# Two graph attention layers on one core: a second form of the second attention, powers for the norms' roots, loops of eight graphs

## What is computed

```python
def layer0(src, adj, ...):
    scores = einsum('bhid,bhjd->bhij', q, k) / sqrt(32)
    attn = softmax(scores, axis=-1)
    out = sum(einsum('bhij,bhjd->bhid', attn * (adj == r), v_r) for r in range(4))
    x = ln(src + out @ Wo + bo, g1, beta1)
    return ln(x + gelu(x @ W1 + b1) @ W2 + b2, g2, beta2)

def layer1(features, adj, Wq, Wk, Wv, Wffn, g1, b1, g2, b2):
    q, k, v = heads(features @ Wq), heads(features @ Wk), heads(features @ Wv)
    e = einsum('whqd,whkd->whqk', q, k)
    e = where(e >= 0, e, 0.2 * e)
    attn = softmax(where(adj[:, None] > 0, e, -9e15), axis=-1)
    h = einsum('whqk,whkd->whqd', attn, v)
    out = ln(h, g1, b1)
    out = ln(concatenate([out, features], axis=-1) @ Wffn.T, g2, b2)
    return out + features
```

## Time and profile before

| | us |
|---|---|
| runs | 3582.01, 3583.69 (median), 3592.45 |
| profiled execution | 3597.16 (its span 3594.9) |
| first attention, from the start to its barrier | 0 to 1250; first matmul 26.50, last output 1239.21 |
| feed-forward | 1250 to 1985 |
| second attention | 1985 to 3594.9, 1610; first matmul 2011.47 |

### The profile page before, as it was taken

One profiled execution on the slowest core, in us unless ns is written; L12 is line 12 of the kernel. 1 busy time (PEld: TensorE's weight loads), 2 busy tenths in 40 slices (PEclk: granted clock), 3 DMA queues, 4 the chain that ended last, 5 costly groups with the idle time before them and its releaser, 6 DMA issues. The chain is left out here.

```text
span 3594.9 us, 96982 instructions
## 1 busy us (share of the span) xinstructions
PE 3085.4 (86%) x31169; PEld 2287.0 (64%) x31169; DVE 2723.2 (76%) x7645; ACT 2427.9 (68%) x5646; POOL 1769.1 (49%) x3716
## 2 busy tenths in 40 slices
PE   5999999999999489999999488878888888788886
PEld 3666666666665256666666377767777777677775
DVE  4888888888888345655555388888888888888886
ACT  2566666666666255555555488888888888888886
POOL 0566666666666425545545034443444444344445
PEclk9999999999999789999999699998999999999998
DMA  3444444444444111111111344443443444344332
GB/s 117 131 133 132 132 132 132 132 132 132 132 132 124 42 47 48 54 52 47 47 47 38 94 113 115 118 114 102 114 119 103 112 115 115 100 113 119 106 109 60
DMA packets 296923, 364.46 MB, mean 101 GB/s; under 512 B 29536, under 2 KB 213728, under 8 KB 296544
## 3 DMA queue, kind: packets, MB, share of 16 engines
q1 hardware_dynamic: 295104, 358.20, 33.6%
q10 hardware_dynamic: 1440, 1.65, 0.1%
HBM read 241.77 MB, written 117.96 MB: 100 GB/s over the span
## 5 line engine op out<-in xcount | busy, mean ns | idle before, releaser
L433 ACT ACTIVATE l_prob<-l_neg_e,l_neg_max 128x256 f32<-128x256 f32 x1024 | 518.0, 522 | 18.0 <-DVE l_neg_max L726 10.2
L726 DVE CUSTOM_DVE_ANT_0 l_neg_e<-l_score,l_leaky 128x256 f32<-128x256 f32 x1024 | 391.7, 420 | 151.0 <-ACT l_prob L433 93.1
L896 PE MATMUL l_tprob<-l_ident,l_prob 128*128 128x128 f32 x2048 | 362.3, 304 | 157.8 <-ACT l_prob L433 146.8
L473 ACT ACTIVATE l_leaky<-l_score 128x512 f32<-128x512 f32 x512 | 307.6, 601 | 219.8 <-PE l_score L912 219.6
L1774 DVE TENSOR_TENSOR f_gl<-f_act,f_gh 128x512 f16<-128x512 f32 x256 | 244.9, 957 | 275.5 <-ACT f_act L1701 275.4
L909 PE MATMUL l_score<-l_stack 128*128 128x256 f16 x1024 | 283.3, 299 | 107.0 <-DMA l_stack<-qk_scratch 106.9
L1696 ACT ACTIVATE f_gh<-f_up,f_b 128x512 f16<-128x512 f32 x256 | 175.5, 685 | 279.1 <-PE f_up L1822 279.0
L1387 DVE TENSOR_TENSOR a_linked<-a_prob,a_mask 128x1024 f32<-128x1024 f32 x256 | 350.2, 1368 | 6.9 <-ACT a_prob L1211 6.9
L732 DVE TENSOR_TENSOR l_pt<-l_tprob,l_pt 128x512 f16<-128x512 f32 x512 | 351.1, 686 | 1.4 <-ACT l_pt L446 1.4
L896 PEld LDWEIGHTS l_tprob<-l_ident,l_prob 128*128 128x128 f32 x2048 | 235.9, 151 | 174.7 <-ACT l_prob L433 130.2
L543 POOL TENSOR_TENSOR l_hl<-l_zt,l_hh 128x512 f16<-128x512 f32 x64 | 74.0, 1156 | 507.6 <-ACT l_hh L493 507.6
(11 more groups left out here) (227 smaller groups left out, 10376.2 us busy)
## 6 DMA issues: line engine op xcount, KB each, us to landing
l_stack<-qk_scratch SPq DMA_DIRECT2D x512, 128.0 KB, 3.1
a_stack<-qk_scratch SPq DMA_DIRECT2D x384, 128.0 KB, 2.8
qk_scratch<-a_qk SPq DMA_DIRECT2D x64, 512.0 KB, 2.8
qk_scratch<-l_qk SPq DMA_DIRECT2D x64, 512.0 KB, 4.7
a_x_sb<-x_t SPq DMA_DIRECT2D x64, 256.0 KB, 2.7
a_adj_sb<-adj_t SPq DMA_DIRECT2D x64, 256.0 KB, 2.8
a_res<-x_nodes SPq DMA_DIRECT2D x64, 256.0 KB, 3.0
after_attention<-a_z_out SPq DMA_DIRECT2D x64, 256.0 KB, 2.1
```

The costliest lines, as they stand in the source:

```text
L433: last = nc.scalar.activation(prob[:, s, i], src[:, i], ACT.Exp, bias=neg_max[:, s, i:i + 1], scale=1.0 if first else -1.0, accum_out=rsum ...
L473: nc.scalar.activation(leaky4[:, s], score[s][:], ACT.Relu, scale=1.0 / ALPHA - 1.0).then_inc(relu_done, 1)
L726: last = nc.vector.tensor_tensor_reduce(neg_e[:, s, i], score[s][:, i], leaky4[:, s, i], -ALPHA, 3e38, ALU.add, ALU.min, neg_max[:, s, i:i ...
L896: last = nc.tensor.transpose(tprob[s][:, jt, it * P:(it + 1) * P], prob[:, s, it, jt * P:(jt + 1) * P], ident[:])
```

## The change

**The second attention** gets its own function `attention_second` (prefix `b_`), in the form of the first attention:

- the stack of 98 rows in a ring of four, with six loads for eight; x in four slots, and xh, xl kept for eight graphs;
- upright scores `score` without the mask; VectorE adds the mask (16-bit, from `adj`) and takes the maximum in one pass (`neg_max`, two instructions of 128x256 a head); no relu on this side;
- per graph `offset` (the maximum with the leaky factor, times 5), turned by TensorE (`turn_max`), split into two 16-bit rows (`max_rows`, times 1/4096), stored and loaded into rows 96 and 97 (`store_m`);
- turned scores `score_t` (`ST`), then a relu with factor 4 in place in PSUM on ScalarE (`relu`), then `add` on TensorE into the same bank: `far` times an identity with 5 * -9e15 (128x512, 16-bit), and the 98 rows again, scores and maximum; then one exponential of 128x512 with factor 0.2 into `prob`, float32;
- `values` and `sums_t` in column tiles, as in the first attention, four groups per graph; `turn_sum`, `rinv`, `turn_heads`, `hs`; 
- for rows without edges: `linked` (from `adj_t`, loaded in addition), `count` (two matmuls with ones), `any`, `far = any - linked` on GpSimd, and `zero_q` (q's halves times `any`, on VectorE, before the store);
- v is kept as float32 (one copy by ScalarE, no halves); `hl` moves from GpSimd to VectorE; the factor g1 is multiplied into `wo` at the start, its bias into a row that is added with `y`.

**The norms** of all three stages: one `ALU.pow` with exponent -0.5 on GpSimd and the product `shift`; VectorE has two small operations behind the statistics in place of five.

**The loop**: U is 8, so the body is eight graphs (eight pairs in the feed-forward) and `2 * U` = 16 are written out ahead of it. x has four slots and the stack a ring of 4 in `attention_first`, as many as before.

```diff
-U = 4
-RSQRT_MAGIC = float(0x5F3759DF)
-NEWTON = 3
+U = 8
...
                 def norm_root(b, k):
...
-                    for _ in range(NEWTON):
-                        for out, a, c in ((s["prod"], s["half"], s["root"]), (s["prod"], s["prod"], s["root"])):
-                            nc.gpsimd.tensor_tensor(out[:], a[:], c[:], ALU.mult).then_inc(root_chain[k], 1)
...
+                    nc.gpsimd.tensor_tensor(s["root"][:], s["var"][:], minus_halves[:], ALU.pow).then_inc(root_chain[k], 1)
+                    pool.wait_ge(root_chain[k], count(b, ROOTS, 1))
                     nc.gpsimd.tensor_tensor(shift[k][:], s["neg_mean"][:], s["root"][:], ALU.mult).then_inc(root_chain[k], 1)
...
-    RING = U
+    RING = 4
+    XS = 4
...
+def attention_second(nc, x_in, x_out, adj, adj_t, w, scr, scr_m, consts):
...
+    AT = {"load": 4, "load_adj": 4, "xT": 8, "xh": 9, "xl": 9, "q": 10, "q_hi": 11, "q_lo": 11, "linked": 8, "k": 12, "k_hi": 13, "k_lo": 13,
+          "count": 9, "any": 9, "v": 14, "v_out": 15, "zero_q": 12, "far": 10, "store_qk": 13, "mask": 16, "S": 17, "max": 17,
+          "offset": 24, "turn_max": 25, "max_rows": 26, "store_m": 26, "ST": 28, "relu": 28, "add": 29, "exp": 29, "values": 33, "res": 45,
+          "evac": 40, "turn_sum": 40, "rinv": 41, "turn_heads": 43, "hs": 43, "stats0": 44, "z1": 45, "turn_z": 46, "hh": 46, "hl": 47,
+          "out_x": 47, "out": 48, "y": 49, "stats1": 50, "z": 52, "affine": 53, "store": 55}
...
+                        sp.dma_start(scr[i].rearrange("k p n -> p k n"), qk[:, i]).then_inc(qk_stored[i], 16)
+                        sp.wait_ge(qk_stored[i], parts_stored)
+                        if stacks_read is not None:
+                            sp.wait_ge(added, stacks_read)
...
+                        nc.scalar.activation(prob[:, he], score_t[s][:].rearrange("p t n -> p (t n)"), ACT.Exp,
+                                             scale=ALPHA).then_inc(exp_done, 1)
...
+                        nc.scalar.activation(score_t[s][:], score_t[s][:], ACT.Relu, scale=SLOPE - 1.0).then_inc(relu_done, 1)
...
+                        for it in range(NT):
+                            col = column(hm, it)
+                            last = nc.vector.tensor_tensor_reduce(junk[:, s, it], score[s][:, it], mask[:, i, it], -1.0, 3e38,
+                                                                  ALU.add, ALU.min, neg_max[:, i, col:col + 1])
...
+                        nc.tensor.matmul(score_t[s][:].rearrange("p t n -> p (t n)"), far_ident[:], far[:, r4].rearrange("p t n -> p (t n)"),
+                                         start=False, stop=False, skip_group_check=True)
+                        for jt in range(NT):
+                            last = nc.tensor.matmul(score_t[s][:, jt], stack[0:KS, r4, 1, a, c * N + jt * P:c * N + (jt + 1) * P],
+                                                    stack[0:KS, r4, 0, a, c * N:(c + 1) * N], start=False, stop=True, skip_group_check=True)
+                        last.then_inc(added, 1)
...
+                        for term in range(2):
+                            for a in range(HQ):
+                                he = HQ * c + a
+                                part = slice(DH * a, DH * (a + 1))
+                                if term:
+                                    last = nc.tensor.matmul(sums_t[part, 0:N], pick[:, c], prob[:, he, cols], start=k == 0, stop=k == 3)
+                                else:
+                                    nc.tensor.matmul(heads_t[part, c], values[:, r4, jt, he * DH:(he + 1) * DH], prob[:, he, cols],
+                                                     start=jt == 0, stop=jt == 1)
...
-    attention_layer(nc, 1, mid2, out, adj, w1, scr1, consts)
+    attention_second(nc, mid2, out, adj, adj_t, w1, scr1, scr_m, consts)
```

728 lines of the change are left out of this document (654 added, 74 removed).

## The result

The changed kernel takes 3394.6 us (median of four runs, 3390.4 to 3399.7) against 3584.8 before (3582.0 to 3592.5): a ratio of 0.947, 95% interval 0.945 to 0.949. That is 190 us less; the prediction said 164 less, 3420 us.

The account below looks back on a forecast made before the run. TensorE bound the first attention and feed-forward; in the second attention no engine was full, TensorE waiting for exponentials and stack. Stages -163, -6 and +5 gave -164: 3433 against the profiled 3597.2, 3420 us as median; range 3340 to 3525.

Parts of the forecast that it names:

- TensorE's sum: Second attention: TensorE's operations, each priced from trace rows, add up to 20.2 us a graph at clock 1.00.
- Late stack: Second attention: TensorE waits 0 to 1.9 us a graph for the stack from scratch memory; 0.6 taken.
- late v: Second attention, step 6 of a graph's eight: v waits 0.4 us for k low.
- The stage's sum: Second attention: start, 64 graphs of 21.2 us, fill and drain, and five branches, together 1447 against 1610 us, -163.
- Start, fill and drain: Second attention: TensorE starts 20 us after the barrier, and filling and draining the pipeline take 45 us.
- -38 for the power: First attention: power in place of Newton's chain saves some 0.6 us a graph over 64 graphs, -38 us.
- xl is then bound by xh: First attention: without Newton's chain xl waits for xh, ending 0.7 us before the chain's end; 0.6 of 0.73 saved.
- +32 in the first attention: First attention, eight-graph body: five branches back of 4 us, +20, and a sometimes late stack, +12.
- +5: Feed-forward with a body of eight: one branch back and its start cost 5 us.
- The second: Rival, both attentions: no late stack, branches of 2 us, second attention's period 20.4 us; 3340 us, chance 0.14.
- The third: Rival: bodies beyond the buffer slow both attentions, +96 in the first, +147 in the second; 3660 us, chance 0.06.
- The fourth: Rival: power takes 3 us or more, so z1 is late in each graph, +1.5 x 64; 3515 us, chance 0.05.
- The first: Rival: the stack binds each graph of the second attention at 22.1 to 22.8 us; say 3500 us, chance 0.18.

Follow-up runs that it names:

- Newton's run: The changed kernel with Newton's chain and its seeds back in the second attention alone, the other stages keeping the power: 3609.5 us.
- the eight loads: The changed kernel with two more loads of the second attention's stack per graph, into rows nothing reads, so eight for six: 3485.8 us.
- the shorter body: The kernel before with two of three products left out of the second attention's values, loop of four, 1310 TensorE instructions for 1820: 3481.0 us.

## Why the prediction was right, step by step

**TensorE's sum** held. 20.2 us were forecast for a graph of the second attention; the window has 20.2 (957.8 over the 47.5 graphs of 21.0 us that 1000 us hold), and as much without a loop (991.5 over 49.2), where a graph takes 20.3 us. The clock of 1.00 came too. Relu in place costs 0.50 us start to start and the power 0.71, both near the value taken:

```profile
2635.59 0.71 POOL L1888 TENSOR_TENSOR b_nw_root<-b_nw_var,b_minus_halves 128x2 f32<-128x2 f32 x1 [13.25 <-DVE b_nw_neg_mean L1961]
...
2637.34 0.60 ACT L1821 ACTIVATE b_prob<-b_score_t 128x512 f32<-128x512 f32 x1 [0.82 <-PE b_score_t L2098]
2637.84 0.59 ACT L1827 ACTIVATE b_score_t<-b_score_t 128x512 f32<-128x512 f32 x1
2638.35 1.08 ACT L1873 ACTIVATE b_z<-b_y,b_shift,b_nw_root 128x256 f32<-128x256 f32 x2
```

**Late stack and late v.** 0.6 and 0.4 were forecast; the rows have 0.3 and nothing. The store was hardly ever late (4 of 48), since a fetch falls into its first 2 us in 2 of 48 graphs. That was luck: the prediction named the fetching at changing places but worked out nothing from it, and in the kernel before the same fetching hit every store.

**The stage's sum** was right by two errors that offset each other. 64 graphs and five branches were 1382 us by the prediction; 64 times the measured mean from y to y (20.60) is 1319, 63 less. In the loop a graph with its share of the branch is 21.0 where the prediction has 21.2 and 0.4: a branch back was priced at 5 us, and TensorE stands 2.3 to 2.7 at it. The rest of the 63 is that the first ten graphs take 20.3 us and the last four 14 to 19. Start, fill and drain were 65 and are 111 (some 5 more, counted from the barrier). The first y comes 121 us behind the stage's first load (105 before), the last 12 us ahead of its end (15 before): the longer pipeline was priced by its steps at full pace, and its start costs more.

**The first attention.** -38 for the power was 36 in the run with the power alone, by another way. The step that failed is "xl is then bound by xh, 0.7 us before the chain's end": one pair of rows was read, and in the graph ahead of it the two lie 0.16 apart. With the chain gone GpSimd waits for xh, and then the four operations ahead of `hl` are what TensorE waits for:

```profile
609.17 1.16 POOL L1285 TENSOR_TENSOR a_xl<-a_x_sb,a_xh 128x512 f16<-128x512 f32 x1 [3.21 <-ACT a_xh L1209]
610.29 1.27 POOL L1297 TENSOR_TENSOR a_resb<-a_res,a_vrow 128x512 f32<-128x512 f32 x1
611.51 2.26 POOL L1309 TENSOR_TENSOR a_z<-a_z,a_vrow 128x512 f32<-128x512 f32 x1
613.86 1.28 POOL L1313 TENSOR_TENSOR a_z_out<-a_z,a_vrow 128x512 f32<-128x512 f32 x1
615.09 2.14 POOL L1276 TENSOR_TENSOR a_hl<-a_heads_n,a_hh 128x512 f16<-128x512 f32 x1
```

The wait on `hl` went from 0.73 to 0.41 us a graph (20.4 over 50). What made up for it was left out of the prediction: the drain. From the last xh to the stage's end it was 112.4 us, and is 97.0 (95.0 with the power alone). There the norms of the last graphs stand behind one another with nothing beside them, and each chain counts in full. TensorE's wait for `hl` in that stretch, before and after:

```profile
PE a_back_bank L1456 <- POOL a_hl L1294: 18.8, 6, 6.4
```

```profile
PE a_back_bank L1428 <- POOL a_hl L1276: 10.7, 5, 4.2
```

**The loop of eight.** +32 in the first attention was five times too much: the loop alone measured +6. A branch back there costs some 2 us (17.6 us from y to y, 19.3 to 19.5 across a branch, up to 1.6 more in the graph behind), not 4, and the stack is not late, as the fetches fall 2 to 3 us behind the store or clear of it (the table above). In the feed-forward +5 measured +4.7 for the loop alone and +2.6 with the power, which a scatter of 2 to 3 us hardly parts. In the second attention the loop was the prediction's largest miss: 40 us were given to it (eight branches fewer, of 5 us), 73 measured, and 112 to 127 lay in the loop of four. By the medians the loop alone took 41 us off, where the prediction's terms for it add up to 3. Since the forecast took the period of the new form from its own sum, and not from the old one's, the miss did not reach the total; a forecast that had scaled the old period would have failed.

**Rivals.** The second (everything overlaps, a period of 20.4, 3340 us) is not what came, with 21.0 in the loop; it is what is left when the loop goes (20.3, 3344.8 us). The third (bodies beyond the buffer slow both attentions) falls: the first attention's code is now fetched, and SP's wait for its store is what it was (120.6 us for 51, against 117.2 for 50 in the earlier trace rows). It had one half right, that the slow store comes with the fetching; but it does so only where a fetch falls into the store. The prediction's case against it, that the store was late in some graphs and not in others, misread the trace: in the kernel before it was late in 40 of 41. The fourth (a slow power) falls by the power's 0.71 us, but its mechanism is close to the one that Newton's run shows, at 3.5 us a graph (224/64). The first stands close by, as the eight loads show. The page "Runtime: NRT & Kernel Launch" of the Trainium skill, section "Instruction fetch mechanics", was cited for bodies beyond TensorE's 2048 instructions; the runs agree in kind (a body of 1310 or 1470 matmuls and weight loads isn't fetched again, those of 1820 and more are, though 1820 is below that figure), and show that what it costs depends on what else is under way: some 6 us in the first attention (loop of eight alone), 105 to 125 in the second.

## What to carry to other kernels

Count the instructions of a loop body on the busiest engine before anything else: a body that just fails to stay at hand may cost more than its branches show, and writing the loop out can then be the larger gain. Look where the fetches fall beside the transfers that something waits for. Price a new form from its own operations, not from the old period, and price start and drain by their own waits, since a latency that costs nothing in the steady part counts in full there. A shorter chain on a side engine is worth what stands behind it: the same power brought 6 to 18 us in one form and 224 in the other.

## What the runs showed of the hardware that was not expected

- A float32 power with exponent -0.5 over 128x2 on GpSimd takes 0.71 us, as much as three and a half products of that size (0.20).
- A multiplication in place of 128x1024 elements of 16 bits on VectorE takes 0.69 us, no more than 128x512 from PSUM (0.68); 0.9 was taken for it:

```profile
2638.48 0.69 DVE L2050 TENSOR_TENSOR b_qk<-b_qk,b_any_link 128x1024 f16<-128x1024 f16 x1
```

- A 512 KB store completes later when the fetch of a block of TensorE's code begins within 2 us behind its issue: a mean of 4.65 us to the first load before, where a fetch fell beside each store, against 2.94 with the shorter body and no fetch. It holds for the old form (58 of 58 such stores in the table's three lines), and in the few cases of the new form and the first attention (5 of 6).
- Straight code is fetched without holding up TensorE (99% busy over 1000 us, 78 blocks), while a branch back to code that isn't at hand costs 2 to 4 us in the changed kernel's attentions (up to 6 with Newton's chain in the second) and some 5 in the old; to code at hand, 2 in the old form.
